# Expert stages of a fused two-layer kernel: token rows brought into slot order through DRAM instead of by one-hot matmuls

## What is computed

```
xn     = layernorm(x)                            # per token
logits = xn @ router_w + router_b                # 8 experts
top2   = top_k(logits, 2); probs = softmax(top2)
pos    = running count of each expert's tokens   # position of a token in its expert
buf[e, pos] += xn                                # 76 slots per expert and batch; over that: dropped
h      = (buf @ w_c_fc + b) ; g = buf @ w_gate + b
y      = (silu(h * g)) @ w_c_proj + b            # 128 -> 512 -> 128 for each expert
x     += sum over the 2 choices of prob * y[e, pos]
```

## Time and profile before

| | |
|---|---|
| median of 3 runs | 2286.04 us (2285.88 to 2286.19) |
| the profiled execution's own time | 2280.57 us |
| its span, first to last instruction | 2278.7 us |
| PE busy | 2170.7 us (95%) |
| DVE busy | 1522.8 us (67%) |
| ACT busy | 1242.7 us (55%) |
| POOL busy | 690.7 us (30%) |
| mean granted TensorE clock | 0.990 of full speed |

### The profile page before, as it was taken

How to read it: one execution, slowest core, us unless ns; L and a number is a source line. 1 busy time by engine, 2 the same in 40 slices (tenths; PEclk the granted TensorE clock), 3 DMA queues, 4 the chain that set the end, 5 groups by cost and what they waited for, 6 DMA issues and landing times. The chain is left out here.

```text
span 2278.7 us, 42519 instructions
## 1 busy us (share of the span) xinstructions
PE 2170.7 (95%) x13706; PEld 1748.3 (77%) x13706; DVE 1522.8 (67%) x4922; ACT 1242.7 (55%) x2504; POOL 690.7 (30%) x724
## 2 busy tenths in 40 slices
PE   5989998999999999899999999999999899999995
PEld 5978888977777777777777777877777777777775
DVE  6867776876777776556565566666666666777664
ACT  4645445754554554465566665666665444545542
POOL 0412222533575655500000000000100344665545
PEclk9999999999999999999999999999999999999998
DMA  8040000000111111200000000000000011111122
GB/s 276 0 176 0 0 0 1 2 10 22 36 41 43 37 38 44 56 7 0 0 0 0 0 0 1 1 1 1 1 1 1 12 28 40 46 51 49 51 55 73
DMA packets 70648, 68.44 MB, mean 30 GB/s; under 512 B 9312, under 2 KB 57952, under 8 KB 70112
## 3 DMA queue, kind: packets, MB, share of 16 engines
q1 hardware_dynamic: 60960, 47.62, 6.6%
q0 software_dynamic: 8192, 16.79, 3.2%
q10 hardware_dynamic: 1344, 2.16, 0.4%
HBM read 32.47 MB, written 34.08 MB: 29 GB/s over the span
## 5 line engine op out<-in xcount | busy, mean ns | idle before, releaser
L2034 ACT ACTIVATE moe_fc<-moe_bank,all_b_fc 128x380 f32<-128x380 f32 (+2 forms) x448 | 245.8, 549 | 277.7 <-PE moe_bank L1964 274.6
L2141 DVE SCALAR_TENSOR_TENSOR moe_act<-moe_bank,all_b_moe_gate,moe_fc 128x380 f32<-128x380 f32 (+2 forms) x448 | 256.7, 576 | 168.3 <-PE moe_bank L1968 101.4
L1980 PEld LDWEIGHTS moe_bank<-all_w_proj,moe_act 128*128 128x128 f32 x2560 | 300.0, 192 | 12.2 <-issue 2.4
L1980 PE MATMUL moe_bank<-all_w_proj,moe_act 128*128 128x128 f32 x2560 | 305.7, 276 | 2.0 <-DVE moe_expert_out L2150 2.0
L1803 POOL DMA_INDIRECT all_landed<-rows_out,all_take_at x256 | 271.7, 1061 | 117.9 <-issue 113.4
L1494 POOL COPY lin_xn_ones<-lin_xn 128x254 f32<-128x254 f32 x32 | 12.7, 398 | 720.7 <-PE lin_bank L1244 720.4
L2041 ACT ACTIVATE moe_act<-moe_act 128x760 f32<-128x760 f32 (+2 forms) x224 | 174.7, 780 | 93.2 <-DVE moe_act L2141 92.7
L1879 POOL TENSOR_SCALAR moe_hot<-all_slot_ids,moe_slot 128x608 fp32r<-128x608 f32 x112 | 203.3, 1824 | 68.3 <-DVE moe_slot L2118 33.7
L1388 ACT ACTIVATE lin_neg<-lin_bank 128x512 f32<-128x512 f32 x256 | 151.7, 592 | 105.5 <-PE lin_bank L1236 61.9
L1286 PEld LDWEIGHTS lin_bank<-lin_kv,lin_qT 128*128 128x128 f32 x1024 | 145.0, 192 | 74.4 <-issue 62.3
L1964 PE MATMUL moe_bank<-gau_rowsT,all_w_fc 128*128 128x380 f32 (+2 forms) x448 | 170.1, 461 | 1.6 <-ACTq L2045 1.6
(11 more groups left out here) (248 smaller groups left out, 4472.8 us busy)
## 6 DMA issues: line engine op xcount, KB each, us to landing
rows_out<-moe_expert_out SPq DMA_DIRECT2D x96, 128.0 KB
rows_out<-all_zeros SPq DMA_DIRECT2D x1, 9728.0 KB, 28.7
rows_out<-moe_expert_out SPq DMA_DIRECT2D x80, 62.0 KB
all_landed<-rows_out,all_take_at POOLq DMA_INDIRECT x256, 2.7
out<-all_x SPq DMA_DIRECT2D x5, 640.0 KB, 4.5
all_w_fc<-in_w_fc SPq DMA_DIRECT2D x1, 2048.0 KB, 9.8
all_w_gate<-in_w_gate SPq DMA_DIRECT2D x1, 2048.0 KB, 13.6
all_w_proj<-in_w_proj SPq DMA_DIRECT2D x1, 2048.0 KB, 18.1
```

Source lines behind the costliest of these rows:

```text
L1980: last = nc.tensor.matmul(bank[OUT][:, j * DIM:(j + 1) * DIM], act_in[:, i % 2, h, j * P:(j + 1) * P], k.w_proj[:, e * MC + h, :], start=( ...
L2034: nc.scalar.activation(fc[:, j, 0:c.width], bank[FC + j % 2][:, 0:c.width], ACT.Identity, bias=k.b_fc[:, e * MC + j:e * MC + j + 1]).then_ ...
L2141: nc.vector.scalar_tensor_tensor(act_in[:, i % 2, j, 0:c.width], bank[GATE + j % 2][:, 0:c.width], k.b_moe_gate[:, e * MC + j:e * MC + j + ...
```

## The change

The one-hot products go. POOL scatters each batch's normalised rows with four indirect DMAs (two token tiles by two choices) into a DRAM buffer of 609 rows, at the row that `assign` gave; a slot past the capacity is out of bounds and isn't written. There are four such buffers, `rows_in`, used in turn. SP waits for the scatters and loads the rows back in slot order (`load`, new at lag 8): per half one DMA of two blocks of 128 rows and one DMA of the last 128 rows of the half, which overlaps the block before it (rows 176 to 303 of 304). PE then transposes the three blocks (`send`). The rows' buffers `parts` and `hot` are replaced by `arrive`; `xn` has four buffers instead of three; the slot numbers are written as integers. `route_step` goes from 5 (9 in the sixth chunk) to 4 (8), and the sends from lags 10 and 11 (mostly 11 and 12) to 14 and 15. The four DRAM buffers are filled with zeros beside `rows_out` in the attention stage before. `RouteAhead` is unchanged.

```diff
+RINGS = 4
...
+                for ring in k.rows_in:
+                    flat = ring.rearrange("r d -> (r d)").rearrange("(p m w) -> p m w", p=P, m=3)
+                    sp.dma_start(flat, k.zeros[:, None, 0:(EXPERTS * CAP + 1) // 3].broadcast_to([P, 3, (EXPERTS * CAP + 1) // 3])).then_inc(k.zeroed, 16)
...
-LAST_PLAN = Plan((4, 5, 5, 5, 5, 5, 3), (5, 5, 5, 5, 5, 9), (None, (11, 5), (11, 5), (11, 5), (11, 5), (11, 5), (15, 4)))
+LAST_PLAN = Plan((4, 5, 5, 5, 5, 5, 3), (4, 4, 4, 4, 4, 8), (None, (11, 5), (11, 5), (11, 5), (11, 5), (11, 5), (15, 4)))
...
-ROUTE_LAGS = {"norm": 0, "transpose": 1, "router": 2, "mask": 3, "count": 4, "assign": 5, "hot0": 8, "hot1": 9,
-              "send0": 10, "send1": 11}
+ROUTE_LAGS = {"norm": 0, "transpose": 1, "router": 2, "mask": 3, "count": 4, "assign": 5, "load": 8, "send0": 14, "send1": 15}
...
+HALF_BLOCKS = -(-HALF // P)
+HALF_WHOLE = (HALF_BLOCKS - 1) * P
...
+                def load(b):
+
+                    sp.wait_ge(scattered[(b - OWN) % RINGS], scattered_at(b))
+                    if b - 2 >= OWN:
+                        sp.wait_ge(sent_ps, 2 * (b - 2) + 2)
+                    ring = k.rows_in[(b - OWN) % RINGS]
+                    for h in range(2):
+                        lo = 1 + h * HALF
+                        sp.dma_start(arrive[:, (b - OWN) % 2, h, 0:HALF_BLOCKS - 1, :],
+                                     ring[lo:lo + HALF_WHOLE, :].rearrange("(j p) d -> p j d", p=P)).then_inc(arrived[(b - OWN) % 2], 16)
+                        sp.dma_start(arrive[:, (b - OWN) % 2, h, HALF_BLOCKS - 1, :],
+                                     ring[lo + HALF - P:lo + HALF, :]).then_inc(arrived[(b - OWN) % 2], 16)
...
+                        if "load" in work:
+                            load(work["load"])
+                        if s % MC == MC - 1 and i:
+                            keep(i - 1)
...
+                def scatter(b):
+                    ring = (b - OWN) % RINGS
                     pool.wait_ge(xn_ready, b + 1)
...
                     pool.wait_ge(routed, b + 1)
+                    if b - RINGS >= OWN:
+                        pool.wait_ge(arrived[(b - OWN) % 2], arrived_at(b - RINGS))
+                    for t in range(TILES):
+                        for h in range(TOP_K):
+                            nc.gpsimd.indirect_dma_start(k.rows_in[ring], bass.IndirectOffsetOnAxis(slot[:, ring, t, h:h + 1], 0),
+                                                         xn[:, b % XN, t, :], None, bounds_check=EXPERTS * CAP,
+                                                         oob_is_err=False).then_inc(scattered[ring], 16)
...
                 def send(b, h):
...
-                        pe.wait_ge(split_done, b + 1)
+                        pe.wait_ge(arrived[(b - OWN) % 2], arrived_at(b))
                     pe.wait_ge(sent_sb, 2 * b + h)
-                    for t in range(TILES):
-                        if h == 0:
-                            pe.wait_ge(hot_sb, TILES * b + t + 1)
-                        for q in range(2):
-                            last = nc.tensor.matmul(bank[SENT][:, 0:HALF], parts[:, b % PARTS, q, t, :],
-                                                    hot[:, b % 2, t, h * HALF:(h + 1) * HALF],
-                                                    start=(t == 0 and q == 0), stop=(t == TILES - 1 and q == 1))
+                    for j in range(HALF_BLOCKS):
+                        at = min(j * P, HALF - P)
+                        last = nc.tensor.transpose(bank[SENT][:, at:at + P], arrive[:, (b - OWN) % 2, h, j, :], k.ident[:, :])
                     last.then_inc(sent_ps, 1)
```

More of the change, by code:

```diff
@@ L1729, in moe_stage @@
         over = k.sb("over", [P, 2, TILES, TOP_K])
[L1730 removed]
+        slot = k.sb("slot", [P, RINGS, TILES, TOP_K], U32)
         prob, take_at, landed = k.prob, k.take_at, k.landed
@@ L1784, in slots_of @@
                 for i, b in enumerate(follow):
-                    later = how.route_step[c.n] == 5 and b != follow[-1]
                     for what, lag in ROUTE_LAGS.items():
-                        work[i * how.route_step[c.n] + lag + (later and what in SENDS)][what] = b
+                        work[i * how.route_step[c.n] + lag][what] = b
             if c.n:
@@ L1843, in store @@
                     sp.dma_start(final[:, lo * TILES:hi * TILES, :], k.x[:, lo * TILES:hi * TILES, :]).then_inc(stored, 16)
[L1845 to L1849, removed]
+                def load(b):
[9 more added lines that the diff above has]
+                                     ring[lo + HALF - P:lo + HALF, :]).then_inc(arrived[(b - OWN) % 2], 16)
+                sp.wait_ge(k.zeroed, 16 * (1 + RINGS))
+                for c, slots in order:
+                    for s, work in slots:
+                        i = c.n * EXPERTS + s // MC
+                        if "load" in work:
+                            load(work["load"])
+                        if s % MC == MC - 1 and i:
+                            keep(i - 1)
+                            if out is not None and (i - 1) % EXPERTS == EXPERTS - 1 and 2 * EXPERTS - 1 <= i - 1:
+                                store(plan[(i - 1) // EXPERTS - 1])
+                keep(UNITS - 1)
                 if out is not None:
@@ L1896, in _ @@
                     for s, work in slots:
-                        if "norm" in work:
-                            split(work["norm"])
                         if "assign" in work:
-                            first_choice(work["assign"])
+                            scatter(work["assign"])
                         if "gather" in work:
@@ L2177, in _ @@
                             assign(work["assign"])
-                        for t in range(TILES):
-                            if f"hot{t}" in work:
-                                second_choice(work[f"hot{t}"], t)
                         if "combine" in work:
@@ L2249, in program @@
         k.slot_ids = k.sb("slot_ids", [P, EXPERTS * CAP])
+        k.rows_in = [nc.dram_tensor(f"rows_in{r}", (EXPERTS * CAP + 1, DIM), F32, kind="Internal").ap() for r in range(RINGS)]
         k.zeroed = k.dma_sem("zeroed")
```

52 lines of the change are left out of this document (15 added, 37 removed).

## The result

| | before | after |
|---|---|---|
| median | 2285.88 us (2280.63 to 2286.19) | 2272.91 us (2268.74 to 2275.58) |
| ratio, 95% interval | | 0.9949 (0.9937 to 0.9962) |
| the profiled execution | 2280.57 us, span 2278.7 | 2268.74 us, span 2266.9 |
| PE busy | 2170.7 us | 2147.8 us |
| DVE busy | 1522.8 us | 1419.8 us |

The change makes the kernel faster by 0.51%, 11.7 us by the means of the five runs and 13.0 by their medians, and that is clear of noise. The forecast was -31 us. The direction is right and the size is not: a good half of the expected gain is missing.

A forecast was written before the change was run, and what follows sets the result against it. PE was taken to bound the kernel: 71.7 us of sends go, 39.8 us of transposes come, 1.0 us of waits goes and 2 us is added, so -31 us from 2286.04 to 2255.0 us. The range was 2244 to 2284 us.

The forecast's parts named there:

- The swap of sends: PE's sends: 112 halves of matmuls at 0.64 us (71.7 us) give way to 336 transposes (39.8 us), gaining 31.9 us.
- at their own duration: Rival at PE's sends: three transposes cost 0.83 us, more than the matmuls, +21 us, 2308 us in all; chance 0.04.
- The scatters' price and the trip to the sends: POOL to PE's sends: scatter 1.06 us, landing 2.7; trip 12.3 to 19.3 us within 20.9, so no wait of PE.
- the rows come too late: Rival at `send0`: slow scatter landings stall PE, an excess paid 22 times; 2 us over gives +13, 2299 us; chance 0.12.
- Waits of `norm`: PE's `transpose` ahead of the router, 8.6 us idle before: 2 us added, as a few batches find DVE ahead no more.
- DVE's relief at nothing: Expert stages: DVE's 94.4 us of comparisons go at no gain, since PE is the cover; at most its 15 us idle.
- more than the sum: Rival in the expert stages: DVE's and POOL's relief gives back part of PE's 15 us idle: -41, 2245 us; chance 0.04.
- POOL's lateness is covered: Fourth gathers of a chunk: some 3 us late for `combine`, covered by PE running about 4.6 us ahead of DVE.
- the rival gave the place: POOL as the bound: fourth gathers late behind two scatter groups, up to 30 us lost, middle 2270 us; chance 0.12.

The follow-up runs named there:

- combines at 15, gathers eight and six: Changed kernel, combines at slots 15, 19, 23, 27, 31, gathers eight slots ahead for a chunk's first three batches, six for the others: 2246.64 us, 0.9838 of the kernel before.
- half the scatters: Changed kernel with the scatters of the second choice left out, so 112 DMAs less on POOL: 2243.69 us, 0.9826 of the kernel before.
- the run with two slots less: Combines at 15, gathers eight and six, with the sends at lags 12 and 13 instead of 14 and 15: 2252.70 us, 0.9864 of the kernel before.
- two versions of the changed kernel: DVE's 112 comparisons put back, results unused, into gathers six ahead (2260.89 us, from 2250.87) and into combines at 15, gathers eight and six (2257.32 us, from 2246.64).
- gathers six ahead: Changed kernel with gathers issued six slots ahead of their combine instead of five: 2250.87 us, 0.9850 of the kernel before.
- the later versions: Changed kernel with gathers six ahead (2250.87 us), or combines at 15 and gathers eight (2247.82 us), eight and six (2246.64 us), or eight and seven ahead (2248.01 us).
- the two runs with gathers six ahead: Changed kernel with gathers six slots ahead instead of five, without DVE's comparisons (2250.87 us) and with the 112 comparisons put back, results unused (2260.89 us).

## Why the prediction was right and wrong

**The swap of sends: right.** Three transposes are followed after 598.63 - 598.31 = 0.32 us, 0.33 as the median of 112; the forecast was 0.355 with 0.33 as its end. By its own terms the swap is then -71.7 + 37.0 = -34.7 us. (Where the prediction says that one `up` takes 0.64 us, it means one of its two products.) In the runs where PE hardly waits the busy time of PE in the stages fell by 31.8 us (combines at 15, gathers eight and six) and 35.2 us (half the scatters). Each transpose lasts 275 ns in its group, and three cost 0.33: the rival "at their own duration" is refuted. The Trainium skill's figure (TensorE: Matmul & The Clock Gate, Part 4: PE-mode transpose, about 275 ns) agrees with that duration, and read as a price it would be wrong by a factor of 2.5.

**The scatters' price and the trip to the sends: right.** A scatter takes 0.99 us on POOL and lands after 2.3 us (forecast 1.06 and 2.7):

```profile
rows_in<-moe_xn,moe_slot POOLq DMA_INDIRECT x224, 2.3
```

Over the 56 batches it is 5.6 to 9.2 us from the slot numbers to the end of the last scatter, then 3.1 to 4.7 us to the last issue of a load. The trip in which this has to fit is 14.1 to 19.2 us, median 17.9, and not the 20.9 of the forecast, since DVE writes the slot numbers later than PE passes their slot. For the batch shown above these rows of DVE and SP stand beside those of POOL and PE: slot numbers at 582.29, the last of its scatters at 590.89, loads issued by 594.34, send at 598.31.

```profile
582.07 0.22 DVE L2127 SCALAR_TENSOR_TENSOR moe_slot<-moe_pos,moe_over 128x4 uint32<-128x4 f32 x1
```

```profile
592.11 0.37 SPq L1861 DMA_DIRECT2D moe_arrive<-rows_in  x1
...
593.85 0.49 SPq L1863 DMA_DIRECT2D moe_arrive<-rows_in  x1
```

No send waited for its load, and the run with two slots less shows that some 15 us are too short for a few. So "the rows come too late" had its place right and did not come about; its price, 22 times an excess, no run shows. One reason against it was read too widely: that every plain transfer of these sizes lands within 3 us holds for the rows it shows, but in the same trace two loads of 64 KB in the set-up landed after 5.2 and 17.9 us.

**Waits of `norm`: sign wrong, small.** The forecast added 2 us at the `transpose` ahead of the router. Its idle time fell from 8.6 to 5.9 us, because DVE was relieved: in the kernel before without DVE's comparisons PE's waits there went from 7.8 to 3.3 us.

**DVE's relief at nothing: wrong by 9 to 12 us.** "PE is the cover, and it had next to no idle time to give back", the prediction said. It had 12.8 us in the stages, and the run on the kernel before shows that 9.0 us of the stages' time go with DVE's comparisons alone; in two versions of the changed kernel they cost 11.1 and 11.9 us of the stages. The prediction's own bound of 15 us held; the value taken within it did not. The rival "more than the sum" had priced this at 10 us.

**The step that failed: POOL's lateness is covered.** "POOL keeps up over a chunk, but a group often stands behind another" was right, and the rival gave the place: the fourth gathers of ten chunks, behind two groups of scatters. It put the lateness at 3 us; DVE's ten waits there are 3.8 to 5.4 us. Then the prediction set it aside, since "PE runs up to two slots ahead of DVE, about 4.6 us, which should cover 3 us". PE does run ahead that far: in the rows above it goes on from 598.63 to 604.20 us, two slots and a `down`. But what holds PE up is not the wait alone. It is the wait with the `combine`, the statistics and the next product behind it: 603.02 to 605.32 us, another 2.3 us. And ACT stands behind it too: PE's next product, at 606.71, waits 0.43 us for `moe_fc`.

What is covered can be read from the time that PE takes from the first `up` of a chunk's seventh unit to the first of the next chunk; the fourth `combine` falls into it. First the changed kernel at the place shown above, where DVE waits 3.83 us, then the run with half of the scatters:

```profile
594.47 0.80 PE L1972 MATMUL moe_bank<-gau_rowsT,all_w_fc 128*128 128x380 f32 x2
...
612.77 0.80 PE L1972 MATMUL moe_bank<-gau_rowsT,all_w_fc 128*128 128x380 f32 x2
```

```profile
804.33 0.81 PE L1972 MATMUL moe_bank<-gau_rowsT,all_w_fc 128*128 128x380 f32 x2
...
811.47 1.26 DVE L1820 SCALAR_TENSOR_TENSOR all_x<-all_landed,all_prob,all_x 128x128 f32<-128x128 f32 x4 [2.42 <-DMA all_landed<-rows_out,all_take_at]
...
821.23 0.80 PE L1972 MATMUL moe_bank<-gau_rowsT,all_w_fc 128*128 128x380 f32 x2
```

It is 18.30 us against 16.90. With gathers six ahead, where DVE does not wait there, it is 16.9 us too. So a wait of 2.4 us is covered, not 4.6, and what goes beyond is paid: 1.41 us more of wait, 1.40 us more of time.

By this measure the ten fourth `combine`s cost the changed kernel 19.4 us. The ten waits at the first `combine`, which the rival didn't have, cost some 6 us more: from slot 8 to slot 16 PE takes 18.54 us in the mean, and 17.93 with half of the scatters. From sum and result the lateness costs -34.7 - 1.0 - 9.0 = -44.7 in the stages against -16.6 measured, so 28 us, or 27 if the relief of 9.0 holds the 1.0 ahead of sends. Half of the scatters gave back 25.7 us of the stages' time, and one slot of lead for the gathers 16.1. The rival's range "up to 30 us" was right; its chance of 0.12 rested on the cover. That its middle, 2270 us, lies near the 2272.9 measured is in part luck: its smaller loss went with a relief of nothing.

So the forecast of -31 was the swap alone. The result is the swap, some 9 us of relief that were left out, and some 25 to 28 us of lateness that was seen and thought covered.

Not settled is what keeps the later versions at -33 to -35 us in the stages, where half of the scatters reached -42.3. Their waits for loads, DVE's waits at the first `combine`, and the slow stretch told at the end are part of it, but were not taken apart.

## What to carry to other kernels

Work in one queue is judged by its longest stretch without a gap ahead of what somebody waits for, not by its sum over a period: here 52 us in 74 were enough to lose more than half of a gain, and one slot of earlier issue won most of it back. A cover is set against the wait together with the work that stands behind it on the waiting engine. And the relief of an engine that is off the path can be worth a good part of the idle time of the one that is on it, here 9.0 us where that was 12.8; a run that leaves that work out of the old kernel measures it.

## What the hardware showed beside this

In the run with gathers six ahead one of PE's two waits for late loads is long, 1.98 us in one piece:

```profile
752.16 0.55 PE L1962 MATMUL moe_bank<-all_ident,moe_arrive 128*128 128x128 f32 x3 [1.98 <-DMA moe_arrive<-rows_in]
```

The stretches around it (columns as in the earlier trace rows; the granted clock is the third number from the end):

```profile
745.00:750.00 5.00, 5.00 (x25) 3.28 (x23) 1.78 (x3) 2.13 (x4) 4.02 (x4) 1.00 0.32 79
750.00:755.00 5.00, 3.02 (x9) 1.61 (x9) 0.61 (x1) 1.85 (x4) 0.00 (x0) 0.77 0.36 101
755.00:760.00 5.00, 5.00 (x33) 4.46 (x32) 2.79 (x8) 1.73 (x3) 0.00 (x0) 0.88 0.00 0
760.00:765.00 5.00, 4.96 (x23) 3.09 (x22) 3.23 (x13) 2.83 (x5) 0.00 (x0) 1.00 0.14 39
```

The granted clock falls to a mean of 0.77 and 0.88, a mix of its two levels of 1.2 and 2.4 GHz, and the unit takes 12.0 us from `down` to `down` instead of 8.5. So here a wait of 2 us in one piece cost more than its length. It need not: in the changed kernel PE waits 1.94 us in one piece for DVE's product, and the clock stays at 1.00.

```profile
1901.49 0.91 PE L1976 MATMUL moe_bank<-moe_rowsT,all_w_gate 128*128 128x380 f32 x2 [1.94 <-DVE moe_act L2144]
```

```profile
1900.00:1905.00 5.00, 3.08 (x11) 1.63 (x12) 3.46 (x9) 2.55 (x5) 0.00 (x0) 1.00 0.13 39
1905.00:1910.00 5.00, 5.00 (x35) 4.18 (x34) 1.33 (x3) 2.93 (x6) 0.00 (x0) 1.00 0.00 0
```

What decides between the two is not shown.

POOL's indirect DMAs are a little slower beside DVE's comparisons: gathers 1.05 us with them and 1.01 without, scatters 1.01 and 0.99, in the two runs with gathers six ahead. The Trainium skill (SBUF — State Buffer, the section on a bandwidth-pool intuition that's wrong, behind the box on the "DVE blocks DMA" trap) gives a DMA that takes about 620 ns alone and 3100 ns beside a DVE `tensor_copy`, five times as long, where the rival of the prediction took three. The two runs here differ on DVE by the comparisons alone, and beside these it is 2 to 4%.
